# A wait on GpSimd between its first eight gathers and the rest, in a DLRM tower kernel

## The reference, cut to what matters

```python
e = jnp.stack([tbl_0[ids[:, 0]], ..., tbl_39[ids[:, 39]]], axis=1)      # (2048, 40, 32)
iidx, jidx = jnp.triu_indices(40, k=1)
z = jnp.einsum('bpd,pde,bpe->bp', e[:, iidx, :], bilinear_matrices, e[:, jidx, :])   # (2048, 780)
h = jnp.concatenate([z, dense_ctx], axis=1)
h = jnp.maximum(h @ W_top1 + b_top1, 0.0)
h = jnp.maximum(h @ W_top2 + b_top2, 0.0)
y = h @ W_top3                                                           # (2048, 1)
```

## Time and profile before

| | before |
|---|---|
| runs | 917.25, 912.99, 911.36 us, median 912.99 us |
| profiled execution, its span | 907.2 us |
| TensorE matmul busy | 797.3 us (88%) |
| VectorE busy | 586.9 us (65%) |
| GpSimd busy | 422.2 us (47%), of it 430 gathers 421.4 us, 980 ns each |
| ScalarE busy | 199.3 us (22%) |
| DMA | 22.53 MB, mean 25 GB/s |

### The profile page before, as it was taken

The page is one execution under the profiler, slowest core; times in us unless marked ns, Lnnn a source line. Parts: engine busy times, 40 slices in busy tenths (PEclk is TensorE's granted clock), DMA queues, the critical chain, the costliest instruction groups (busy, mean ns, idle before and its releaser), DMA issues.

```text
span 907.2 us, 16013 instructions
## 1 busy us (share of the span) xinstructions
PE 797.3 (88%) x6766; PEld 318.0 (35%) x6766; DVE 586.9 (65%) x702; ACT 199.3 (22%) x362; POOL 422.2 (47%) x437
## 2 busy tenths in 40 slices
PE   3213888777789999999999999999999999999999
PEld 1001344333333333333233232333323324445446
DVE  3002767554458787988676787886877879657550
ACT  4001232110232121232322102323221021322111
POOL 7771346666655665655564556555522333220000
PEclk9555889987889999999999999999999999999999
DMA  4201663300020101010201010102000000000000
GB/s 83 36 14 23 119 85 85 66 13 11 12 34 11 29 12 34 11 29 11 34 11 26 11 33 11 28 10 23 10 14 5 19 7 15 7 6 1 2 1 1
DMA packets 62562, 22.53 MB, mean 25 GB/s; under 512 B 45283, under 2 KB 61677, under 8 KB 62490
## 3 DMA queue, kind: packets, MB, share of 16 engines
q1 hardware_dynamic: 48702, 14.37, 7.4%
q0 software_dynamic: 13760, 7.07, 6.5%
q10 hardware_dynamic: 28, 0.06, 0.0%
HBM read 21.40 MB, written 0.07 MB: 24 GB/s over the span
## 4 chain that ended last, share of the span: by engine, by line
PE 75%; another core or an unknown queue 10%; issue 9%; ACT 3%; DVE 2%; DMA 0%; DVEq 0%; ACTq 0%
PE U L832 23%; PE bank_z L857 19%; PE misc L883 15%; PE misc L783 11%; PE U L841 3%; PE U L806 2%; PE U L883 1%; DVE prod L731 1%; ACT x_twin L568 1%; PE bank_z L865 1%; ACT x_look L550 1%; ACT x_T L541 0%; ACT x_T L550 0%; DVE ones L695 0%
## 5 line engine op out<-in xcount | busy, mean ns | idle before, releaser
L499 POOL DMA_INDIRECT rows<-in_tbl,idx x430 | 421.4, 980 | 382.0 <-PE bank_z L857 241.7
L731 DVE TENSOR_TENSOR prod<-U,x_T 128x1024 f32<-128x1024 f32 (+1 forms) x314 | 343.6, 1129 | 115.6 <-PE U L832 85.4
L857 PE MATMUL bank_z<-prod,select 128*32 128x512 f32 (+1 forms) x2000 | 226.3, 536 | 5.7 <-ACT z L530 4.8
L832 PE MATMUL U<-x_T,W 32*128 32x512 f32 (+1 forms) x1440 | 206.3, 559 | 19.5 <-ACT x_T L541 11.9
L783 PE MATMUL misc<-ones,tabs 125*32 125x512 bf16 (+1 forms) x1890 | 142.7, 367 | 58.5 <-issue 58.1
L695 DVE TENSOR_SCALAR ones<-idx_wide,row_of 125x2048 bf16<-125x2048 f16 (+3 forms) x180 | 106.9, 623 | 97.4 <-remote 70.9
L783 PEld LDWEIGHTS misc<-ones,tabs 125*32 125x32 bf16 x1890 | 70.1, 102 | 147.8 <-issue 119.6
L832 PEld LDWEIGHTS U<-x_T,W 32*128 32x128 f32 x1440 | 82.1, 190 | 108.2 <-issue 55.4
L731 DVE TENSOR_TENSOR prod<-U,x_look 128x1024 f32<-128x1024 f32 (+1 forms) x90 | 88.2, 1005 | 46.5 <-PE U L832 39.5
L883 PE MATMUL misc<-z,W 128*128 128x512 f32 (+1 forms) x238 | 107.3, 565 | 0.4 <-ACT x_look L550 0.4
L857 PEld LDWEIGHTS bank_z<-prod,select 128*32 128x32 f32 x2000 | 47.9, 111 | 153.3 <-issue 108.9
(11 more groups left out here) (70 smaller groups left out, 285.0 us busy)
## 6 DMA issues: line engine op xcount, KB each, us to landing
rows<-in_tbl,idx POOLq DMA_INDIRECT x430
idx_wide<-idx_rows SPq DMA_DIRECT2D x6, 500.0 KB
idx_wide<-idx_rows SPq DMA_DIRECT2D x6, 375.0 KB
idx_wide<-idx_rows SPq DMA_DIRECT2D x3, 187.5 KB
W<-in_W_top SPq DMA_DIRECT2D x35, 2.0 KB
W<-_L_rec_bilinear_matrices SPq DMA_DIRECT2D x4, 128.0 KB
W<-in_W_top SPq DMA_DIRECT2D x1, 512.0 KB
idx_wide<-idx_rows SPq DMA_DIRECT2D x2, 250.0 KB
```

The lines of the kernel that those rows point to most:

```text
L499: nc.gpsimd.indirect_dma_start(out=rows[:, n % R_SLOTS, t, f, :], out_offset=None, in_=tables[field][:, :], in_offset=bass.IndirectOffsetO ...
L731: last = nc.vector.tensor_tensor(to[:, :, m * N:(m + n) * N].rearrange("p r (m n) -> p r m n", m=n), U[:, at:at + 2, m * N:(m + n) * N].re ...
L832: last = nc.tensor.matmul(U[:, at + r % 2, m * N:(m + 1) * N], W[row, at_W:at_W + P], x_of(o, a)[row, :], start=True, stop=True, skip_grou ...
L857: last = nc.tensor.matmul(bank_z[r * DIM:(r + 1) * DIM, 0:N], sel, prod[:, (2 * g + r // 2) % P_SLOTS, r % 2, m * N:(m + 1) * N], start=(k ...
```

## The change

In GpSimd's program a wait is put ahead of turn 1. The eight gathers of turn 0 are issued as before; then GpSimd waits until the first look-up is copied, and after that goes on with the other 48 gathers of block 0 and all later ones. No other engine's program is changed.

```diff
             for n, (o, c) in enumerate(TURNS):
+                if n == 1:
+                    pool.wait_ge(misc_kept, JOB[("look", 0, 0)] + 1)
                 if n >= R_SLOTS:
                     pool.wait_ge(turned, n - R_SLOTS + 1)
                 for f in GATHERED[(o, c)]:
```

## The result

The changed kernel took 900.64, 903.62, 897.30 and 903.72 us, median 902.13, beside 912.62 us (median of four) for the kernel before. The ratio of the runs is 0.9866, 95% interval 0.983 to 0.990: 1.3% faster. Forecast were 902.5 us and a gain of 10.5. The profiled execution has a span of 898.8 us, 8.4 less than that of the kernel before.

A forecast was written before the change was run, and what follows sets the result against it. Gathers were taken to hold TensorE at the start, 1.405 us each, with TensorE alone setting the pace after 257 us. Span 907.2 - 10.5 = 896.7, plus 5.8 for the median, gives 902.5 us; range 888 to 917.

The forecast's parts named there:

- What bounds the kernel: At the start each gather holds TensorE's signals 1.405 us; from 257 us to the end TensorE's matmuls set the pace.
- Step 1: First look-up behind only eight gathers: done at 20.9 us, GpSimd goes on at about 21.3, 63.6 us earlier.
- Step 2: The other 48 gathers, issued from 21.3 to 81.3 us, hold TensorE until 88.7; some 53 us go back.
- Step 3: TensorE between 21.3 and 88.7 us: 128 instructions signalled, just past turn c=3 at release, a gain of 10.5 us.
- Step 4: After the release both kernels run the same list, so the 10.5 us stay to the end.
- 5.8 us: Amount by which the median time lies over the span, added to 896.7 to give 902.5 us.
- SyncE at nothing: Loads behind SyncE's held load start about 62 us earlier, beside the 48 gathers; costed at nothing, 5 us if wrong.
- E: Rival: gathers don't cause the crawl; look-up still ends at 84.55, 7.2 us lost, time 920; chance 11%.
- B: Rival: lighter hold in the second gather run, 0.20 us an instruction throughout; gain 15 to 21, time 895; chance 14%.
- D: Rival: hold outlasts gathers by 8.1 us, second hold to 95.9; 3.5 us slower to 3.3 faster; chance 13%.
- C: Rival: no hold in the second burst, gathers pace block 0; gain near 50, time about 863; chance 5%.

## Why the prediction was right, step by step

**What bounds the kernel: right.** The price of 1.405 us a gather held everywhere the crawl showed: (86.35 - 18.34) / 48 = 1.417 in the kernel after, 1.42 and 1.44 in the others. The stretch from 257 us on, busy 99%, was called TensorE's own pace, and that is nearly so: the same 3929 matmuls take 485.7 us with the crawl and 469.7 without it. But 10.4 of the 16 us between them are recorded as busy time (479.86 against 469.48), at a granted clock of 1.00 in both, so a busy TensorE in the earlier trace rows doesn't exclude that it is slowed a little. What was won ahead of the stretch was kept: the lead is 9.0 us at the 190th gather and 8.4 at the end.

**Step 1 (look-up 63.6 us earlier): right, a little short.** It was 66.9 (17.68), 0.6 of it because indices and tables landed earlier in this execution (the 16 matmuls of L903 begin at 11.78, not 12.43). I took 0.059 us a matmul from the end of a crawl, at a granted clock of 0.53; the look-up in the kernel after kept TensorE busy and was granted 1.00: 114 matmuls began within 4.18 us, less than 0.037 each.

**Step 2 (hold to 88.7): right.** It began 3 us earlier, at 18.34, and ended at 86.4.

**Step 3 (TensorE at its turn c=3 when let go): right place by a wrong count.** I counted 128 instructions signalled by then. In truth 88 were signalled by 36.8, within 18.5 us (turns c=1 and 2, projects 0 and 1), 0.21 us each, and for the following 49.5 us no signal that VectorE or ScalarE waited for arrived, though TensorE began a matmul about each 2.8 us. The paces of 0.32 to 1.37 us, read from a first stretch in which the signals happened to fall so, don't carry over; the run of the same kernel in another job had quite different ones. What saved the sum is the other half of the step: work begun ahead is released at once. Turn c=3 was signalled at 86.6 against 99.4 before, a lead of 12.8 us.

**Step 4 (nothing is lost after): wrong by 3.6 us.** At the first sum the lead of 12.8 had shrunk to 9.2 (93.53 against 102.77), and at the 57th gather too. Here is the place, kernel after, then kernel before:

```profile
88.47 3.18 PE L834 MATMUL U<-x_T,W 32*128 32x256 f32 x16 [12.26 <-DVE prod L733]
...
91.58 1.90 PE L859 MATMUL bank_z<-prod,select 128*32 128x256 f32 x16
```

```profile
99.90 1.42 PEld L832 LDWEIGHTS U<-x_T,W 32*128 32x128 f32 x16 [0.71 <-ACT x_T L541]
99.90 1.82 PE L832 MATMUL U<-x_T,W 32*128 32x256 f32 x16 [0.47 <-ACT x_T L541]
```

Project 2 waits for VectorE, whose one-hot tile and four products (86.37 to 89.5) were released only with turn c=3, while in the kernel before the tile and the products were started at 97.4 to 99.9, beside the end of the look-up, and project 2 waited last for ScalarE's copy. And after the crawl, in which it was busy 8.51 of 49.5 us, TensorE has the half clock: granted 0.50 from 86 to 90 us and 0.56 in the window of the restart, against 1.00 in the kernel before at that place, and the 16 matmuls take 3.18 us for 1.82, the sum 1.90 for 1.07. 1.4 us of waiting, 1.4 and 0.8 of clock make the 3.6. An error in the other direction hid most of it: the hold ended 2.3 us earlier than forecast, since step 1 was shorter.

**The number: luck.** That 902.13 us is within half a us of the 902.5 forecast says little, with an interval of the ratio from 0.983 to 0.990 (9 to 16 us). The forecast added 5.8 us to a span of 896.7; measured are 898.8 and a median 3.3 above it. The 5.8 was not a fixed cost: each execution of which both are on record takes 1.8 us more than its span (900.64 against 898.8), and the rest is then that the profiled execution of the kernel before was faster than the median, which no record shows directly. Where the gain comes from was forecast rightly; steps 1 and 4 missed by 3.3 and 3.6 us, in opposite directions.

**SyncE at nothing: right.** The loads now run beside the gathers (DMA share 0.44 in the crawl), and a gather still takes 0.94 us and holds 1.42.

**The rivals.** E had the crawl independent of the gathers: the look-up at 17.68 refutes it. By the rule of the Trainium skill quoted there ("SBUF — State Buffer", section Who interferes with whom), DMA never contends with a compute engine and TensorE waits for no one. In the jobs without the crawl the traces agree (the look-up copied at 18.1 to 19.5 us under running gathers). In those with it the measurement contradicts that TensorE waits for no one (a matmul about each 2.8 us until the gathers are worked off), and decides; that DMA traffic is what it waits for isn't shown, and the empty window from 75 to 80 us speaks against it. B (0.20 us an instruction throughout) was right for the first 18.5 us and wrong for the 49.5 behind them. D (hold outlasting the last gather by 8 us; its second hold comes to 96.3 by its own terms, not 95.9) falls: after eight gathers nothing was late at 13.7, and after sixteen, the last of them issued at 24.3, the hold ended at 26.2. C, no hold of the second burst, is false in this job but true in others. There the sign of its gain was wrong: where there is no hold, the kernel before takes 776 us and so can't have crawled either, and the wait costs 0.7%. I had treated the crawl as a property of the kernel.

**What stays open** is what the crawl comes from: its two ends are shown to follow the gathers' start and number, and spacing them 1.44 instead of 1.25 us apart loosened it in one execution. Not shown is why it is there in some jobs, what a gather occupies for 1.4 us, and whether rows or instructions pay it.

## What to carry to other kernels

Before explaining a stall by the program, time the unchanged program again in other jobs: here the same kernel takes 776 or 912 us, and an edit that helps in one case hurts in the other. A hold that a stream of work lays on another engine is moved by reordering, not removed; count when it lets go (number of items by a price that repeats in the trace), and then who stands ready at that moment, on every engine and at which clock. And of an early lead, forecast only the part that passes the next place where both sides wait for each other.

## What the runs showed of the hardware that was not expected

- The crawl (signals of TensorE seen late while GpSimd issues gathers) is not always there. Without it the kernel before takes 776 to 777 us in four jobs, with it 903 to 912 in three; gathers are 0.95 us long and 1.25 us apart in both. The chip's number doesn't decide it: jobs on a chip numbered 3 were once of one kind and once of the other (if that is one and the same chip, which the records don't say).
- Where it is there, the signals of TensorE are seen late while its instructions still begin, up to three steps of a look-up (72 instructions) ahead.
- It costs most at the start: of 119 us, 44 up to the first sum and 60 in the next 1660 matmuls. Behind them, where TensorE is busy 99% either way, it still costs 16 us on 3929 matmuls, 10 of them recorded as busy time.
- The hold goes on without DMA traffic: in the kernel before no packet ran from 75 to 80 us, and TensorE's matmuls still began 2.8 and 1.4 us apart.
- Setting gathers 1.44 instead of 1.25 us apart let TensorE begin 360 instead of 89 matmuls between 2.9 and 73.5 us under the crawl (one execution).
